# VectorE makes the low part of every weight unit in the GNN groups and Wout

## The chip, the cores and the metric

The kernel runs on one core of a Trainium2 chip, as one program. The metric is the device time of one execution in microseconds (us). The core has five engines with queues of their own: TensorE (PE), VectorE (DVE), ScalarE (ACT), Pool (GpSimd) and the DMA queue of SyncE (SP). They meet only through semaphores.

## The reference

One layer on 384 nodes of 1024 features: a graph attention and a mixing attention run side by side on the same normalised input, and then an attention whose q, k and v come from tree-routed feedforward networks.

```python
xn = layernorm(x)
# gnn: q, k, v = xn @ wq.T + bq ...; q2, k2, v2 = q @ wiq.T + biq ...  (16 heads of 64)
#      softmax(q2 k2^T / 8 + mask(edges)) v2, then @ wo.T + bo
# mix: qkv = xn @ Wqkv; softmax(dots * spiky_weights) v, then @ Wout + bout
x = x + gnn(xn, edges) + mix(xn)
# ffn: three hard-routed trees of 16 leaves give q, k, v; softmax(q k^T / 32) v
x = x + ffn(layernorm(x))
```

## The kernel before

Every matrix product is made from parts of higher and lower significance: an operand a is held as a_hi, a copy rounded to the matmul's input type, and a_lo = a - a_hi, and `product`, `gemm_T` and `gemm_N` add hi*hi, hi*lo and lo*hi.

The weights are a stream of 68 units of 1 MB (128 partitions x 2048 values, 256 output columns each), numbered in the order of use: 24 for the mix groups and the first GNN projections, U_GNN = 24 to 35 for the GNN's second projections (K, Q, V of four groups of four heads), U_OUT = 36 to 39 for Wout, 40 to 43 for wo, and U_FFN = 44 on. Each passes through two-deep buffers, slot n % 2:

- SyncE loads `raw[n % 2]` once the low part of unit n - 2 is made (L335).
- ScalarE's `split_hi(n)` writes `w_hi[n % 2]` (L474); it waits for the load and until TensorE is done with unit n - 1.
- `split_lo(n)` writes `w_lo[n % 2]` = raw - w_hi, on VectorE (L785) for most units, on Pool (L398) for the seven units in ON_POOL: 28, 29, 31, 32, 34, 35 and 37. Two semaphores count, w_lo_ready and w_lo_pool; `lo_turn(n)` is the place of unit n in its count.
- TensorE waits for it in `unit_ready`.

The order of each engine's work is written out by hand. A GNN group gi (0 to 3) begins with the V unit n = U_GNN + 3 gi + 2, and then has four heads. For each head TensorE makes scores (s_bank, L1337), VectorE the masked scores and their maxima (L899, `maxima`), ScalarE the exponentials (L548, `exps`), VectorE the division by the sum (L886, `normals`), TensorE transposes of the three tiles into two banks t_bank (L1346), ScalarE pT_hi (L562) and VectorE pT_lo (L919) from them, and TensorE the product with v (o_bank, L1357), which ScalarE (L570) and VectorE (L850, `join`) bring to o_acc. Between these TensorE makes the K unit n + 1 and the Q unit n + 2 of the next group (in group 3 units 36 and 37 of Wout). `transposes(2)`, the third tile of a head, is issued in the middle of a unit's tile and waits until pT_lo of the first tile has freed its bank of t_bank. `take_K` and `take_Q` bring a unit's results to k_st, q_st and q_lo (ScalarE L498 and L511, VectorE L829 and L841). In group 3 VectorE's `keep_N` copies the results of Wout to y_acc (L964).

ScalarE's order in a group is: exps of head 0, split_hi(n + 1), take_V, exps of head 1, take_V, pT_hi of head 0, exps of head 2, split_hi(n + 2), o_acc of head 0, pT_hi of head 1, exps of head 3, take_K, o_acc, pT_hi of head 2, split_hi(n + 3), take_Q, and so on. VectorE's is the one that the diff shows.

Pool splits the attention outputs beside that: `split_mix(0)` to `(3)`, a cast (L404) and a subtraction (L405) each, and `split_gnn(0)` to `(3)`, two bias additions (L413), a cast (L416) and a subtraction (L417) each, where split_gnn(0) waits until TensorE has done unit 34. Behind split_gnn(2) it issues the loads of bo_b, bout_b, node_raw and b2 (L435 to L438), behind the last head's join the loads of x into x1 (L441); then split_gnn(3), bo_b + bout_b (L445), x1 + bo_b (L447), x1 + y_acc (L450), which sets x1_ready. ScalarE waits for the bias loads before it makes node_hi (L717) and then w_hi of unit 39; VectorE waits for x1_ready, behind split_lo of unit 41 and node_lo (L1120), before it adds the results of wo to x1 (L1129).

Of the kernel before, what the change touches and what calls it, by code (L numbers as in the profile page):

```python
# [24 lines left out]
ALU = mybir.AluOpType  # L25
# [39 lines left out]
def chain_unit(u):  # L65

    return U_A0 if u == 0 else mix_v((u - 1) // 3) + (1, 2, 4)[(u - 1) % 3] if u < 10 else mix_v(3) + u - 9


ON_POOL = (U_GNN + 4, U_GNN + 5, U_GNN + 7, U_GNN + 8, U_GNN + 10, U_GNN + 11, U_OUT + 1)  # L70


def lo_turn(n):

    return sum((u in ON_POOL) == (n in ON_POOL) for u in range(n))


LN_FILLS = KT
# [86 lines left out]
def pv_gnn(g, h):  # L165
    return Index(PV_GNN0 + 4 * g.base + h, g.it, 4 * g.step)
# [24 lines left out]
def program(nc, x, wstream, ecols, pp_in, table, w1m, w2m, bo, bout, nodes, b2, out):  # L191
    with ExitStack() as ctx:
# [12 lines left out]
        def sem(name):  # L205
            return ctx.enter_context(nc.semaphore(name))
# [74 lines left out]
        table_set, table_in, edge_out = sem("table_set"), sem("table_in"), sem("edge_out")  # L281
        raw_in = [sem("raw_in0"), sem("raw_in1")]
        consts_ready = sem("consts_ready")
        w_hi_ready, w_lo_ready, w_lo_pool = sem("w_hi_ready"), sem("w_lo_ready"), sem("w_lo_pool")
        o_half = sem("o_half")
        g_full = sem("g_full")
        g_hi = sem("g_hi")
# [27 lines left out]
        def flat(a):  # L315
            return a.rearrange("p a b -> p (a b)")
# [7 lines left out]
        @block.sync  # L324
        def _(sp):
            for t in range(NT):
                sp.dma_start(x_sb[:, t, :], x[t * P:(t + 1) * P, :]).then_inc(x_in, 16)
            for s in range(2):
                sp.dma_start(raw[:, s, :], wstream[s]).then_inc(raw_in[s], 16)
            for n in range(2, UNITS):  # L330
                if n - 2 in ON_POOL:
                    sp.wait_ge(w_lo_pool, lo_turn(n - 2) + 1)
                else:
                    sp.wait_ge(w_lo_ready, lo_turn(n - 2) + 1)
                sp.dma_start(raw[:, n % 2, :], wstream[n]).then_inc(raw_in[n % 2], 16)  # L335
            for t in range(NT):
                sp.wait_ge(out_ready, 2 * (t + 1))
                sp.dma_start(out[t * P:(t + 1) * P, :], out_sb[:, t, :]).then_inc(out_done, 16)
            sp.wait_ge(out_done, 16 * NT)
# [3 lines left out]
        def _(pool):  # L343
# [49 lines left out]
            pool.wait_ge(g_full, fill_of(Index(mix_v(3) + 1)).value())  # L393
            pool.dma_start(mask8[:, :, :], table.rearrange("(t p m) a -> p t (m a)", t=NT, p=P)).then_inc(table_in, 16)

            def split_lo(n):
                pool.wait_ge(w_hi_ready, n + 1)
                nc.gpsimd.tensor_tensor(flat(w_lo[n % 2][:, :, :]), raw[:, n % 2, :], flat(w_hi[n % 2][:, :, :]),  # L398
                                        ALU.subtract).then_inc(w_lo_pool, 1)

            def split_mix(c):

                both = slice(2 * c, 2 * c + 2)
# [17 lines left out]
            pool.wait_ge(g_full, fill_of(Index(U_GNN)).value())  # L421
            split_mix(0)
            split_mix(1)
            split_lo(U_GNN + 4)
            split_mix(2)
            split_mix(3)
            for n in (U_GNN + 5, U_GNN + 7, U_GNN + 8, U_GNN + 10, U_GNN + 11):
                split_lo(n)
            pool.wait_ge(g_full, fill_of(Index(U_GNN + 11)).value())
            split_gnn(0)  # L430
            split_lo(U_OUT + 1)
            split_gnn(1)
            split_gnn(2)
            pool.wait_ge(g_full, fill_of(Index(U_OUT)).value())
# [339 lines left out]
        def _(dve):  # L774
# [296 lines left out]
            for gi in range(GROUPS):  # L1071
                g = Index(gi)
                n = Index(U_GNN + 3 * gi + 2)
                more = gi < GROUPS - 1
                maxima("gnn", g, 0)
                if gi:
                    join(Index(gi - 1), HG - 1, pv_gnn(Index(gi - 1), HG - 1))
                normals("gnn", g, 0)
                split_lo(n + 1)
                take_V(n, 0)  # L1080
                maxima("gnn", g, 1)
                take_V(n, 1)
                normals("gnn", g, 1)
                take_pT(lambda t: t_gnn(g, 0, t))
                maxima("gnn", g, 2)
                normals("gnn", g, 2)
                join(g, 0, pv_gnn(g, 0))
                if not more:
                    keep_N(n + 1, 0)
                take_pT(lambda t: t_gnn(g, 1, t))  # L1090
                maxima("gnn", g, 3)
                if more:
                    for m in range(2):
                        take_K(n + 1, m, C_BIK + 2 * (gi + 1))
                else:
                    keep_N(n + 1, 1)
                normals("gnn", g, 3)
                join(g, 1, pv_gnn(g, 1))
                take_pT(lambda t: t_gnn(g, 2, t))
                if not more:  # L1100
                    split_lo(n + 3)
                if more:
                    take_Q(n + 2, 0, C_BIQ + 2 * (gi + 1))
                else:
                    keep_N(n + 2, 0)
                join(g, 2, pv_gnn(g, 2))
                take_pT(lambda t: t_gnn(g, 3, t))
                if more:
                    take_Q(n + 2, 1, C_BIQ + 2 * (gi + 1))
                else:  # L1110
                    keep_N(n + 2, 1)
# [126 lines left out]
        def _(pe):  # L1238
# [7 lines left out]
                return last  # L1246

            def unit_ready(n):
                if n.it is None and n.base in ON_POOL:
                    pe.wait_ge(w_lo_pool, lo_turn(n.base) + 1)  # L1250
                else:
                    pe.wait_ge(w_lo_ready, n.value(1, lo_turn(n.base) + 1 - n.base))

            def taken(f):

# [467 lines left out]
```

## Time and profile before

| | before |
|---|---|
| median of 3 runs | 860.81 us (858.89 to 865.01) |
| profiled execution | 865.43 us, span from first to last instruction 863.7 us |
| mean granted TensorE clock | 0.972 |
| PE busy | 786.6 us, 91% |
| DVE busy | 491.7 us, 57% |
| ACT busy | 375.9 us, 44% |
| POOL busy | 172.3 us, 20% |

The span is that of the profiled execution; 1.7 us of its time lie around it. The shares are means over stages: the mix groups end near 340 us, the GNN groups run to about 524, the output projections to about 587, and the FFN to the end.

### The profile page before, as it was taken

To read this page: it belongs to the slowest core of one execution; us is meant where nothing else is said; L and a number is where in the kernel's file an instruction comes from. 1 tells how busy PE (TensorE), PEld (TensorE's weight loads), DVE (VectorE), ACT (ScalarE), POOL (GpSimd) and SP (SyncE) were. 2 spreads that over 40 slices of the span, in tenths; PEclk is the share of its full clock that TensorE was granted. 3 is DMA by queue.
4 is the path that set the end of the run, shared out by engine and by line. 5 is a ranking of instruction groups with operands and counts; after the bars stand their busy time and mean duration, and the time that the engine had idled before them with its cause. 6 is when DMAs were issued, how large, how long until landed. Compare 5 with 4: busy or idle time off the path is not lost.

```text
span 863.7 us, 12450 instructions
## 1 busy us (share of the span) xinstructions
PE 786.6 (91%) x4838; PEld 747.2 (87%) x4838; DVE 491.7 (57%) x1055; ACT 375.9 (44%) x649; POOL 172.3 (20%) x136
## 2 busy tenths in 40 slices
PE   1888999999999799879888998897999999999997
PEld 1778999999999799878788997895898998999995
DVE  5466774774784576757565675645543453364313
ACT  2443655555555446556657552122333333242310
POOL 3201232222322201150403368700000000000000
PEclk9998999999999899999999999898999999999999
DMA  5212122222222222121121217221232233223001
GB/s 210 93 54 94 49 98 99 98 98 98 98 98 98 77 98 98 50 79 69 49 98 49 98 50 243 93 103 44 98 132 112 98 116 129 97 103 142 0 1 74
DMA packets 13956, 79.57 MB, mean 92 GB/s; under 512 B 3168, under 2 KB 3456, under 8 KB 5184
## 3 DMA queue, kind: packets, MB, share of 16 engines
q1 hardware_dynamic: 10656, 74.45, 23.7%
q0 software_dynamic: 2960, 4.26, 1.7%
q8 instruction: 35, 0.57, 0.3%
q10 hardware_dynamic: 288, 0.14, 0.1%
q14 instruction: 17, 0.14, 0.1%
HBM read 76.66 MB, written 2.19 MB: 91 GB/s over the span
## 4 chain that ended last, share of the span: by engine, by line
PE 48%; DMA 22%; DVE 11%; ACT 9%; issue 7%; POOL 2%; POOLq 0%; SPq 0%; ACTq 0%; DVEq 0%
PE g_bank L1274 28%; DMA edge_table<-ew,eidx 20%; PE g_bank L1301 9%; ACT p_ring L548 3%; ACT w_hi L474 3%; DVE w_lo L785 2%; ACT q_st L511 2%; PE g_bank L1245 2%; PE s_bank L1245 1%; PE t_bank L1346 1%; DVE pT_lo L919 1%; DVE p_ring L886 1%; DVE k_st L829 1%; DVE q_lo L841 1%; PE g_bank L1320 1%
## 5 line engine op out<-in xcount | busy, mean ns | idle before, releaser
L1274 PE MATMUL g_bank<-act_hi,w_hi 128*128 128x384 f32 x640 | 228.0, 356 | 6.9 <-DVE k_st L829 3.6
L1274 PE MATMUL g_bank<-act_hi,w_lo 128*128 128x384 f32 x640 | 218.5, 341 | 0.0
L1274 PE MATMUL g_bank<-act_lo,w_hi 128*128 128x384 f32 x640 | 218.2, 341 | 0.0
L785 DVE TENSOR_TENSOR w_lo<-raw,w_hi 128x2048 fp32r<-128x2048 f32 x61 | 147.9, 2425 | 41.2 <-ACT w_hi L474 40.6
L474 ACT ACTIVATE w_hi<-raw 128x2048 fp32r<-128x2048 f32 x68 | 129.6, 1905 | 39.0 <-PE g_bank L1301 38.9
L1274 PEld LDWEIGHTS g_bank<-act_hi,w_hi 128*128 128x128 f32 x640 | 123.8, 193 | 11.8 <-issue 9.9
L1274 PEld LDWEIGHTS g_bank<-act_lo,w_hi 128*128 128x128 f32 x640 | 123.7, 193 | 0.0
L1274 PEld LDWEIGHTS g_bank<-act_hi,w_lo 128*128 128x128 f32 x640 | 123.2, 192 | 0.0
L388 POOL DMA_INDIRECT edge_table<-ew,eidx x51 | 60.3, 1182 | 153.1 <-DMA edge_table<-ew,eidx 150.0
L919 DVE TENSOR_TENSOR pT_lo<-t_bank,pT_hi 128x384 fp32r<-128x384 f32 x96 | 50.4, 552 | 38.8 <-ACT pT_hi L562 30.5
L1346 PE MATMUL t_bank<-ident,p_ring 128*128 128x128 f32 x288 | 43.3, 277 | 27.8 <-DVE pT_lo L919 24.9
L562 ACT ACTIVATE pT_hi<-t_bank 128x384 fp32r<-128x384 f32 x96 | 43.6, 489 | 50.2 <-PE t_bank L1346 49.7
L1346 PEld LDWEIGHTS t_bank<-ident,p_ring 128*128 128x128 f32 x288 | 33.9, 142 | 34.4 <-issue 20.9
L398 POOL TENSOR_TENSOR w_lo<-raw,w_hi 128x2048 fp32r<-128x2048 f32 x7 | 32.1, 4591 | 114.3 <-ACT w_hi L474 114.3
L1301 PE MATMUL g_bank<-w_hi,act_hi 128*128 128x256 f32 x192 | 54.5, 284 | 0.0
L1301 PE MATMUL g_bank<-w_hi,act_lo 128*128 128x256 f32 x192 | 54.3, 283 | 0.0
L1301 PE MATMUL g_bank<-w_lo,act_hi 128*128 128x256 f32 x192 | 54.2, 283 | 0.0
L552 ACT ACTIVATE p_ring<-s_bank,small 128x384 f32<-128x384 f32 x48 | 31.9, 669 | 30.2 <-DVE small L905 30.2
L1274 PE MATMUL g_bank<-h_hi,w_hi 128*128 128x384 f32 x128 | 44.7, 349 | 0.0
L886 DVE TENSOR_SCALAR p_ring<-p_ring,small 128x384 f32<-128x384 f32 x96 | 41.9, 437 | 3.4
L1274 PE MATMUL g_bank<-h_hi,w_lo 128*128 128x384 f32 x128 | 43.0, 336 | 0.0
L1274 PE MATMUL g_bank<-h_lo,w_hi 128*128 128x384 f32 x128 | 42.8, 334 | 0.0
(226 smaller groups left out, 1571.8 us busy)
## 6 DMA issues: line engine op xcount, KB each, us to landing
raw<-wstream_dram SPq DMA_DIRECT2D x68, 1024.0 KB, 4.8
x_sb<-x_dram SPq DMA_DIRECT2D x3, 512.0 KB, 5.0
x<-x_dram POOLq DMA_DIRECT2D x3, 512.0 KB, 6.5
out_dram<-out_sb SPq DMA_DIRECT2D x3, 512.0 KB, 2.6
edge_table<-ew,eidx POOLq DMA_INDIRECT x51, 2.2
edge_table<-mask POOLq DMA_DIRECT2D x1, 576.0 KB, 5.4
mask<-edge_table POOLq DMA_DIRECT2D x1, 576.0 KB, 4.3
bo_b<-bo_dram POOLq DMA_DIRECT2D x1, 512.0 KB, 5.5
```

The costliest lines, as they stand in the source:

```text
L388: nc.gpsimd.indirect_dma_start(table, bass.IndirectOffsetOnAxis(ap=eidx[:, e:e + 1], axis=0), ew[:, e:e + 1], None, bounds_check=N * N - 1 ...
L398: nc.gpsimd.tensor_tensor(flat(w_lo[n % 2][:, :, :]), raw[:, n % 2, :], flat(w_hi[n % 2][:, :, :]), ALU.subtract).then_inc(w_lo_pool, 1)
L474: nc.scalar.activation(flat(w_hi[s][:, :, :]), raw[:, s, :], ACT.Copy).then_inc(w_hi_ready, 1)
L548: ins = nc.scalar.activation(tile, tile, ACT.Exp, bias=nbias[:, s:s + 1], scale=-1.0, accum_out=esum[:, s:s + 1])
L552: ins = nc.scalar.activation(tile, s_bank[q.slot(3)][:, 0:N], ACT.Exp, bias=nbias[:, s:s + 1], scale=alpha[:, c:c + 1], accum_out=esum[:, ...
L562: nc.scalar.activation(pT_hi[:, :, t * P:(t + 1) * P], t_bank[f.slot(2)][:, 0:N].rearrange("p (m n) -> p m n", n=P), ACT.Copy).then_inc(t_ ...
L785: V.tensor_tensor(flat(w_lo[s][:, :, :]), raw[:, s, :], flat(w_hi[s][:, :, :]), ALU.subtract) \
L886: V.tensor_scalar(ring[:, slot, :], ring[:, slot, :], rsum[:, slot:slot + 1], None, ALU.mult) \
L919: V.tensor_tensor(pT_lo[:, :, cols], t_bank[f.slot(2)][:, 0:N].rearrange("p (m n) -> p m n", n=P), pT_hi[:, :, cols], ALU.subtract).then_i ...
L1274: last = mm(out, w2[a], x2[b], start=k == 0 and a + b == 0, stop=not after and k == KT - 1 and a == 1)
L1301: last = mm(out, x2[a], w2[b], start=k == 0 and a + b == 0, stop=not after and k == KT - 1 and a == 1)
L1346: last = nc.tensor.transpose(t_bank[f.slot(2)][:, m * P:(m + 1) * P], p_ring[:, q.slot(PR), m * P:(m + 1) * P], ident[:, :])
```

## The change

Pool no longer makes any low part. ON_POOL, `lo_turn`, w_lo_pool and Pool's `split_lo` are gone. VectorE gets two calls in each GNN group: `split_lo(n + 2)` behind the normals of head 2 and ahead of the join of head 0, and `split_lo(n + 3)` behind pT_lo of head 2, which it had in group 3 only. SyncE and TensorE wait for one count, w_lo_ready. Pool's other work keeps its order and its waits.

```diff
--- before.py
+++ after.py
@@ -65,14 +65,6 @@
 def chain_unit(u):
 
     return U_A0 if u == 0 else mix_v((u - 1) // 3) + (1, 2, 4)[(u - 1) % 3] if u < 10 else mix_v(3) + u - 9
-
-
-ON_POOL = (U_GNN + 4, U_GNN + 5, U_GNN + 7, U_GNN + 8, U_GNN + 10, U_GNN + 11, U_OUT + 1)
-
-
-def lo_turn(n):
-
-    return sum((u in ON_POOL) == (n in ON_POOL) for u in range(n))
 
 
 LN_FILLS = KT
@@ -281,7 +273,7 @@
         table_set, table_in, edge_out = sem("table_set"), sem("table_in"), sem("edge_out")
         raw_in = [sem("raw_in0"), sem("raw_in1")]
         consts_ready = sem("consts_ready")
-        w_hi_ready, w_lo_ready, w_lo_pool = sem("w_hi_ready"), sem("w_lo_ready"), sem("w_lo_pool")
+        w_hi_ready, w_lo_ready = sem("w_hi_ready"), sem("w_lo_ready")
         o_half = sem("o_half")
         g_full = sem("g_full")
         g_hi = sem("g_hi")
@@ -328,10 +320,7 @@
             for s in range(2):
                 sp.dma_start(raw[:, s, :], wstream[s]).then_inc(raw_in[s], 16)
             for n in range(2, UNITS):
-                if n - 2 in ON_POOL:
-                    sp.wait_ge(w_lo_pool, lo_turn(n - 2) + 1)
-                else:
-                    sp.wait_ge(w_lo_ready, lo_turn(n - 2) + 1)
+                sp.wait_ge(w_lo_ready, n - 1)
                 sp.dma_start(raw[:, n % 2, :], wstream[n]).then_inc(raw_in[n % 2], 16)
             for t in range(NT):
                 sp.wait_ge(out_ready, 2 * (t + 1))
@@ -393,11 +382,6 @@
             pool.wait_ge(g_full, fill_of(Index(mix_v(3) + 1)).value())
             pool.dma_start(mask8[:, :, :], table.rearrange("(t p m) a -> p t (m a)", t=NT, p=P)).then_inc(table_in, 16)
 
-            def split_lo(n):
-                pool.wait_ge(w_hi_ready, n + 1)
-                nc.gpsimd.tensor_tensor(flat(w_lo[n % 2][:, :, :]), raw[:, n % 2, :], flat(w_hi[n % 2][:, :, :]),
-                                        ALU.subtract).then_inc(w_lo_pool, 1)
-
             def split_mix(c):
 
                 both = slice(2 * c, 2 * c + 2)
@@ -421,14 +405,10 @@
             pool.wait_ge(g_full, fill_of(Index(U_GNN)).value())
             split_mix(0)
             split_mix(1)
-            split_lo(U_GNN + 4)
             split_mix(2)
             split_mix(3)
-            for n in (U_GNN + 5, U_GNN + 7, U_GNN + 8, U_GNN + 10, U_GNN + 11):
-                split_lo(n)
             pool.wait_ge(g_full, fill_of(Index(U_GNN + 11)).value())
             split_gnn(0)
-            split_lo(U_OUT + 1)
             split_gnn(1)
             split_gnn(2)
             pool.wait_ge(g_full, fill_of(Index(U_OUT)).value())
@@ -1084,6 +1064,7 @@
                 take_pT(lambda t: t_gnn(g, 0, t))
                 maxima("gnn", g, 2)
                 normals("gnn", g, 2)
+                split_lo(n + 2)
                 join(g, 0, pv_gnn(g, 0))
                 if not more:
                     keep_N(n + 1, 0)
@@ -1097,8 +1078,7 @@
                 normals("gnn", g, 3)
                 join(g, 1, pv_gnn(g, 1))
                 take_pT(lambda t: t_gnn(g, 2, t))
-                if not more:
-                    split_lo(n + 3)
+                split_lo(n + 3)
                 if more:
                     take_Q(n + 2, 0, C_BIQ + 2 * (gi + 1))
                 else:
@@ -1246,10 +1226,7 @@
                 return last
 
             def unit_ready(n):
-                if n.it is None and n.base in ON_POOL:
-                    pe.wait_ge(w_lo_pool, lo_turn(n.base) + 1)
-                else:
-                    pe.wait_ge(w_lo_ready, n.value(1, lo_turn(n.base) + 1 - n.base))
+                pe.wait_ge(w_lo_ready, n.value(1, 1))
 
             def taken(f):
```

## Rows read from the trace of the kernel before

**Rows 1.** Waits of TensorE in 336 to 560 us: sum, times, longest, in us.
```profile
PE t_bank L1346 <- DVE pT_lo L919: 18.5, 13, 2.9
...
PE g_bank L1301 <- DVE y_acc L964: 3.2, 1, 3.2
PE g_bank L1301 <- DVE x L1129: 2.9, 1, 2.9
```

**Rows 2.** The page's groups by line: Pool's w_lo (busy us, mean ns | idle before).
```profile
L398 POOL TENSOR_TENSOR w_lo<-raw,w_hi 128x2048 fp32r<-128x2048 f32 x7 | 32.1, 4591 | 114.3 <-ACT w_hi L474 114.3
```

**Rows 3.** Timelines of ScalarE, VectorE and TensorE in group 2: start, duration, [idle before].
```profile
455.10 1.90 ACT L474 ACTIVATE w_hi<-raw 128x2048 fp32r<-128x2048 f32 x1
...
457.54 0.55 DVE L850 TENSOR_TENSOR o_acc<-o_bank,o_acc 64x384 f32<-64x384 f32 x1 [1.70 <-ACT o_acc L570]
458.06 1.02 DVE L919 TENSOR_TENSOR pT_lo<-t_bank,pT_hi 128x384 fp32r<-128x384 f32 x2
...
458.77 0.52 PE L1346 MATMUL t_bank<-ident,p_ring 128*128 128x128 f32 x3 [0.21 <-DVE pT_lo L919]
```

**Rows 4.** The same place in groups 0, 1, 3; last, one window (0.83: granted clock).
```profile
365.90 1.02 DVE L919 TENSOR_TENSOR pT_lo<-t_bank,pT_hi 128x384 fp32r<-128x384 f32 x2
...
367.28 0.49 PE L1346 MATMUL t_bank<-ident,p_ring 128*128 128x128 f32 x3
...
408.76 1.90 ACT L474 ACTIVATE w_hi<-raw 128x2048 fp32r<-128x2048 f32 x1
...
412.12 1.02 DVE L919 TENSOR_TENSOR pT_lo<-t_bank,pT_hi 128x384 fp32r<-128x384 f32 x2
...
413.63 0.49 PE L1346 MATMUL t_bank<-ident,p_ring 128*128 128x128 f32 x3
...
505.20 0.52 PE L1346 MATMUL t_bank<-ident,p_ring 128*128 128x128 f32 x3 [0.61 <-DVE pT_lo L919]
...
400.00:410.00 10.00, 7.97 (x41) 7.68 (x39) 7.25 (x30) 6.43 (x17) 0.00 (x0) 0.83 0.26 101
```

**Rows 5.** Group 0 behind head 2, ScalarE and VectorE.
```profile
379.04 1.92 ACT L474 ACTIVATE w_hi<-raw 128x2048 fp32r<-128x2048 f32 x1
...
383.23 1.25 DVE L841 SCALAR_TENSOR_TENSOR q_lo<-g_bank,pp,q_st 64x384 fp32r<-64x384 f32 x2 [3.62 <-ACT q_st L511]
```

**Rows 6.** Timeline of Pool, from the end of the mix groups on.
```profile
345.07 1.85 POOL L405 TENSOR_TENSOR oTm_lo<-o_acc,oTm_hi 128x768 fp32r<-128x768 f32 x1
...
484.10 1.86 POOL L417 TENSOR_TENSOR oTg_lo<-o_acc,oTg_hi 128x768 fp32r<-128x768 f32 x1
...
502.98 4.61 POOL L398 TENSOR_TENSOR w_lo<-raw,w_hi 128x2048 fp32r<-128x2048 f32 x1 [17.02 <-ACT w_hi L474]
...
516.29 3.75 POOL L417 TENSOR_TENSOR oTg_lo<-o_acc,oTg_hi 128x768 fp32r<-128x768 f32 x1
...
521.16 0.54 POOL L437 DMA_DIRECT2D node_raw<-nodes_dram  x1
...
526.58 2.47 POOL L413 TENSOR_SCALAR o_acc<-o_acc,pp 128x384 f32<-128x384 f32 x2
...
536.31 8.75 POOL L447 TENSOR_TENSOR x<-x,bo_b 128x3072 f32<-128x3072 f32 x1
...
545.84 6.84 POOL L450 TENSOR_TENSOR x<-x,y_acc 128x3072 f32<-128x3072 f32 x1 [0.78 <-DVE y_acc L964]
```

**Rows 7.** Timeline of VectorE: operations from SBUF to SBUF.
```profile
350.37 2.29 DVE L785 TENSOR_TENSOR w_lo<-raw,w_hi 128x2048 fp32r<-128x2048 f32 x1 [1.19 <-ACT w_hi L474]
...
508.76 0.83 DVE L886 TENSOR_SCALAR p_ring<-p_ring,small 128x384 f32<-128x384 f32 x1
...
515.46 2.90 DVE L785 TENSOR_TENSOR w_lo<-raw,w_hi 128x2048 fp32r<-128x2048 f32 x1 [1.24 <-ACT w_hi L474]
...
547.21 7.62 DVE L785 TENSOR_TENSOR w_lo<-raw,w_hi 128x2048 fp32r<-128x2048 f32 x1 [1.52 <-ACT w_hi L474]
...
554.75 1.38 DVE L1120 TENSOR_TENSOR node_lo<-node_raw,node_hi 128x384 fp32r<-128x384 f32 x1
```

## Prediction

> **What bounds the kernel now.** I read the page first, for where TensorE is not busy, then the waits of TensorE between 336 and 560 us, which is where the seven moved operations lie, and then the timelines of the four engines around each of them. Over the whole span TensorE is 91% busy (the table of the profile section has the shares), but in this stretch its longest sum of waits, 18.5 us in 13 waits, is for VectorE's pT_lo, the last link before the transposes may reuse a bank of t_bank; 3.2 us and 2.9 us are single waits in the two output projections [rows 1]. What the reader is to see: the GNN groups are not bound by matmuls alone. They run at the pace of a chain that goes transposes, ScalarE, VectorE, back to TensorE, and every microsecond that is put in front of a pT_lo moves what follows. The operation that changes hands takes 4.59 us on Pool, seven times, 32.1 us in all; VectorE's own takes 2.29 us when nothing disturbs it [rows 2, 7]. Pool is busy for 20% of the span, so the work that it sheds is worth something only where Pool itself is late. That is in one place, the end of this stretch (below).
>
> **The change part by part.** VectorE gets 7 x 2.29 = 16.0 us of work. The value of w_lo is ready 0.04 + 2.29 us after w_hi instead of 0.1 + 4.6 us, but no row of the waits shows TensorE waiting for one of Pool's seven w_lo, nor SP's next load being late for ScalarE, so the shorter operation by itself gives nothing.
>
> *Three splits behind the third pT_lo of head 2 (units 29, 32, 35).* In group 0 ScalarE ends w_hi at 379.04 + 1.92 = 380.96 and VectorE's next work starts only at 383.23, after an idle time of 3.62 us, because it waits for q_st [rows 5]. The split fits into it: 381.00 + 2.29 = 383.29, so 0.06 us, in three groups 0.1 us. The cover is ScalarE's q_st; without it each would cost 2.3 us. I count zero.
>
> *Four splits behind the normals of head 2 (units 28, 31, 34, 37).* Here VectorE is idle too, but for 1.70 us, and it waits for ScalarE's w_hi and then its 0.5 us o_acc. In group 2 w_hi ends at 455.10 + 1.90 = 457.00, VectorE's join starts at 457.54 and its pT_lo at 458.06, and TensorE, which has waited 0.21 us, goes on at 458.77, 0.71 us after pT_lo started [rows 3]. The split can't use that idle time, since it waits for the same w_hi. It starts when w_hi ends and holds VectorE for 2.29 us, where the join came after 0.54 us: join, keep_N, and both pT_lo move by 2.29 - 0.54 = 1.75 us. Queued behind it are join (ScalarE doesn't wait for it), pT_lo (TensorE's transposes wait), and the maxima of head 3. TensorE has little to spare against that:
> - group 2: it waits already, so the whole 1.75 us.
> - group 3: it waits 0.61 us already [rows 4], the whole 1.75 us.
> - group 0: pT_lo from 365.90 to 367.65, transposes possible at 368.36 instead of 367.28 [rows 4]: 1.08 us.
> - group 1: w_hi ends at 410.66; with the 1.06 us of group 2 and the 1.75 us, pT_lo starts at 413.47 instead of 412.12 and the transposes at 414.18 instead of 413.63 [rows 4]: 0.55 us.
> The last two are smaller because TensorE came late itself, in group 1 with the granted clock at 0.83 in 400 to 410 us [rows 4]. Sum 5.1 us. Behind each comes a chain (transposes, pT_hi, pT_lo, maxima, exps, k_st, the next pT_lo) on whose links TensorE waits again in the same group, so I let all of it through. Ends: 0 us if slack swallows them, 7.0 us if all four cost 1.75.
>
> *Pool's other work moves forward.* Two blocks do. split_mix(2) and (3) no longer wait for w_hi of unit 28 and run right behind split_mix(1), which ends at 345.07 + 1.85 = 346.92, to 352.4 (some 2.75 us each: a cast like the 0.8 us one of split_gnn and the subtraction); split_gnn(1) and (2) no longer stand behind the w_lo at 502.98 and follow split_gnn(0), which ends at 484.10 + 1.86 = 485.96, so they run from 486 to 497 [rows 6]. There they meet VectorE operations between SBUF operands. What this costs is seen at 508 to 520. A VectorE w_lo that comes while Pool is at work waits for the end of Pool's instruction and then goes first: 2.90 us instead of 2.29, and Pool's next takes 3.75 us instead of 1.86. The extreme is at 547.21, where w_lo takes 7.62 us, 5.3 more, until Pool's 6.84 us addition is over. A normal (L886) took 0.83 us against 0.42 [rows 6, 7].
> The Trainium skill, page "SBUF — State Buffer", section "Who interferes with whom", says that the two share a port pair, locked for a whole instruction. For w_lo the trace agrees (the 3.75 and 7.62 us).
> In group 0 the normals have 1.19 us of idle behind them before w_lo at 350.37 [rows 7], which takes up most: 0.2 us (0 to 1.9, the latter if Pool's 1.85 us subtraction gets ahead of w_lo). In group 3 the normals before w_lo of unit 36 and w_lo itself lose 0.6 us, the normals of head 1 about 3 x 0.3 us: 1.5 us (0 to 3.5). In return that overlap leaves 508 to 520: w_lo of unit 38 is 0.6 us shorter there, and TensorE waits for what comes behind it: -0.6 us.
>
> *Delay D of TensorE when the last head ends:* 5.1 + 0.2 + 1.5 - 0.6 + 0.1 = 6.3 us.
>
> *What Pool gives back.* bo_b, bout_b and node_raw are issued at about 498 instead of up to 521.16 [rows 6]. Before, ScalarE waits for node_raw before it makes w_hi of unit 39, w_lo follows, y_acc is queued behind w_lo, and TensorE waits 3.2 us for y_acc [rows 1]. That wait goes. What is late next is Pool. Its x1 loads wait for the last join, which is D later, and behind them stand split_gnn(3), from 526.58, the two bias additions (the long one from 536.31 to 545.06) and the addition of y_acc, to 552.68 [rows 6]. This chain moves by D and has only 0.78 us of idle time in it, which now goes, as y_acc is 3.2 us earlier against it. But the earlier w_lo of units 39 and 41 get between Pool's operations at other points and cost it up to 2 us. Then x1_ready comes between 551.7 + D and 553.7 + D. VectorE's node_lo, before at 554.75 with 1.38 us [rows 7] since it was behind the long w_lo, is next, and the x1 addition after it; TensorE restarts at about 554.9 + D, before at 556.79 [rows 1, 6]. So of 6.1 us of waits only 1.9 us are won (0.3 to 2.4); TensorE then waits some 6 us there.
>
> Net: 6.3 - 1.9 = +4.4 us. From there on the FFN is unchanged. The profiled execution took 865.43 us (span 863.7), so it becomes 869.8; the median of the three runs is 860.81, which gives **865.2 us**. With their spread, 858.89 to 865.01, no change and a change of under 1% (8.6 us) can hardly be told apart.
>
> **The rivals.**
> *The waits go and the splits are free.* If something I don't see covers the four splits (TensorE's matmuls could absorb 1 us here and there, as in groups 0 and 1), D is about zero and the net is -1.9 us, at best -6.1 us if both waits of the output projections vanish: 858.9, down to 854.7. For it: VectorE is only 57% busy, and two of four splits meet a late TensorE. Against: 13 waits for exactly that tile.
> *Slower through the clock.* In 400 to 410 us, which begins with one of the 13 waits, the granted clock was 0.83 of the full 2.4 GHz, so it stood for a third of these 10 us on its lower level of 1.2 GHz, and 1.7 us of full speed were lost [rows 4]. The waits before the transposes of head 1 grow to 1.1, 2.0 and 2.4 us in groups 0, 2 and 3. If each brings such a stretch, 3 x 1.7 = 5.1 us come on top: +9.5 us, 870.3. It decides where these waits get as long as the longest of the present ones, 2.9 us [rows 1]. Against: there are 13 waits of 1.4 us on average in this stretch already, and the mean clock over the span is still 0.972.
> *Slower through the whole lock.* If a normal is held for the whole of a Pool instruction and Pool and VectorE take turns, each normal costs up to one Pool operation (1.25 to 1.85 us) instead of 0.3, w_lo of unit 27 and 36 come 3 us later each, and the next normals 2.5 us: 8.5 us instead of 1.7, net +11.2 us, 872.0. This is what the Trainium skill says, page "SBUF — State Buffer", section "Who interferes with whom", of `tensor_scalar` in a two-port mode. Against: 0.83 us is the longest of 96 [rows 7], and Pool's own L413 took 2.47 us [rows 6], as otherwise.
>
> **How the numbers follow.** Forecast 0.63, free splits 0.13, clock 0.14, lock 0.10. The forecast's own range is 862 to 869.5 (D from 4.4 to 9). The range that leaves out no more than 2 in 10 takes in most of the first rival and of the clock: 859 to 872. Faster by over 1% (below 852.2) is beyond every case: 0.02. Slower by over 1% (above 869.4): the lock, two thirds of the clock, a tail of the forecast: 0.23. Within: 0.75.
>
> **What would show it.** Right: seven more w_lo on VectorE of 2.3 us; in groups 2 and 3 the wait before the transposes of head 1 grows by some 1.7 us; q_lo behind the other three doesn't move; split_gnn(1) and (2) at about 486 to 497 relative to their group, node_raw landed long before w_hi of unit 39, no wait for y_acc, one wait of about 6 us for L1129. Wrong: if TensorE's wait for pT_lo in the stretch doesn't grow from 18.5 us, the main term is wrong; if x1_ready no longer sets the end of the projections, the gain is up to 6 us; if normals take over 1 us, the lock; if the granted clock over the span falls from 0.972, the clock.

## The result, and the profile after

The changed kernel takes 869.29 us (median of 8 runs, 867.56 to 870.98), the kernel before 861.41 us (8 runs, 856.14 to 865.01): ratio 1.0096, 95% interval 1.0069 to 1.0123. It is slower by 7.9 us, between 5.9 and 10.6. The forecast was 4.4 us. The profiled execution took 868.51 us with a span of 866.8 us and a mean granted clock of 0.978; over the eight runs the clock lies between 0.970 and 0.978, with a median of 0.974.

The page after, busy times and the groups of w_lo and of the normals:

```profile
PE 781.0 (90%) x4838; PEld 741.3 (86%) x4838; DVE 514.1 (59%) x1062; ACT 375.5 (43%) x649; POOL 141.0 (16%) x129
...
L765 DVE TENSOR_TENSOR w_lo<-raw,w_hi 128x2048 fp32r<-128x2048 f32 x68 | 162.6, 2391 | 45.1 <-ACT w_hi L454 44.5
...
L866 DVE TENSOR_SCALAR p_ring<-p_ring,small 128x384 f32<-128x384 f32 x96 | 44.8, 467 | 3.4
```

Pool is 31.3 us less busy and VectorE 22.4 us more, although seven splits of 2.29 us are only 16.0 us. The rest is mainly node_lo (7.08 us for 1.38) and the normals (44.8 us for 41.9), which stand behind operations of Pool. The waits of TensorE in 336 to 570 us, as in [rows 1]:

```profile
PE t_bank L1323 <- DVE pT_lo L899: 26.4, 15, 3.6
PE g_bank L1278 <- DVE x L1109: 5.5, 1, 5.5
PE g_bank L1251 <- DVE v_st L798: 1.9, 1, 1.9
```

The wait for pT_lo has grown from 18.5 to 26.4 us, a wait of 1.9 us for v_st is new, the one for y_acc (3.2) is gone, and the one for the x1 addition has grown from 2.9 to 5.5 us.

Where the time went is easiest read from borders in VectorE's timeline: the first L899 (L879 after) of each group, the last join and the first addition to x1. Between them, in us, for the profiled executions of all kernels (the tail is from the last join to the first addition to x1; e1 to e12 are the experiments below, and "split" stands for one split_lo):

```
                 group 0  group 1  group 2  group 3   tail    span
before             46.06    46.35    45.88    39.29   32.46   863.7
after              48.78    46.78    46.79    42.69   30.10   866.8
e1 four splits     50.45    46.80    46.83    43.22   30.10   873.5
e2 three splits    46.55    45.16    45.16    38.66   32.48   862.5
e3 Pool held       46.68    46.81    46.80    40.35   30.10   863.3
e4 split later     48.53    45.34    46.51    43.04   30.09   865.9
e5 held + later    49.01    46.53    45.34    41.90   30.10   862.1
e6 early loads     46.54    45.15    45.18    38.68   30.10   858.9
e7 four twice      51.47    49.73    49.49    46.81   30.09   879.9
e8 three twice     51.08    50.65    50.98    42.68   30.11   878.7
e9 clear           46.20    46.53    46.51    41.81   30.10   865.9
e10 Pool chain     45.90    46.34    45.16    39.24   28.78   856.3
e11 w40 first      46.09    46.35    45.15    38.67   28.15   853.5
e12 later alone    46.30    46.50    45.33    39.28   32.47   859.7
```

Two readings matter. Against the profiled execution of before the four groups lose 7.5 us and the tail gives back 2.4; outside them after is 2.0 us shorter, in stages that the change doesn't touch, so the spans differ by 3.1 us only. And that execution of before was itself held up. In e6, whose groups 1 and 2 are those of before, they take 45.15 and 45.18 us, and in e2 45.16; in before 46.35 and 45.88 us, with a stretch of 3.4 us at the lower clock of 1.2 GHz in each. The windows of e6 (group 1) and of before (in group 1):

```profile
392.20:437.30 45.10, 38.57 (x254) 37.10 (x253) 28.72 (x87) 27.76 (x57) 9.17 (x2) 1.00 0.19 71
```

```profile
406.00:409.40 3.40, 3.40 (x13) 3.40 (x12) 3.29 (x16) 2.45 (x7) 0.00 (x0) 0.50 0.03 7
```

The third number from the end is the granted clock. Such a stretch is not wholly chance. e10, e11 and e12 have one at the same place of group 1 (46.34, 46.35 and 46.50 us), e2 and e6 have none there, and in group 0 all five kernels that leave unit 28 to Pool (before, e2, e6, e10, e11) have one, so that an undisturbed group 0 of theirs is in no trace.

Against 45.16 us for an undisturbed group the change costs 3.6 us in group 0, 1.6 in 1 and in 2. Against the 38.67 us of e2, e6 and e11 it costs 4.0 in group 3, and the tail gives back 2.4: 8.4 us, which is inside the measured interval. For group 0 the 45.16 us are an estimate, taken from groups 1 and 2.

**The four splits at the border of head 2.** Group 2 after, VectorE and TensorE, to be held against [rows 3]:

```profile
459.37 2.29 DVE L765 TENSOR_TENSOR w_lo<-raw,w_hi 128x2048 fp32r<-128x2048 f32 x1 [1.19 <-ACT w_hi L454]
461.58 0.54 DVE L830 TENSOR_TENSOR o_acc<-o_bank,o_acc 64x384 f32<-64x384 f32 x1
462.05 1.00 DVE L899 TENSOR_TENSOR pT_lo<-t_bank,pT_hi 128x384 fp32r<-128x384 f32 x2
...
462.73 0.52 PE L1323 MATMUL t_bank<-ident,p_ring 128*128 128x128 f32 x3 [1.83 <-DVE pT_lo L899]
```

VectorE waits 1.19 us for w_hi, then the split stands before join and pT_lo, and TensorE's wait is 1.83 us where it was 0.21. In group 1 the wait is 1.85 us where there was none, in group 3 it is 2.31 where it was 0.61. In group 0 it is only 0.27, because a stretch at the lower clock (0.50 in 360.8 to 364.2 us) lies just ahead and TensorE comes late itself; in e3, which has no such stretch there, it is 1.83.

**The three behind head 2.** Group 0 after, VectorE, against [rows 5]:

```profile
382.90 2.29 DVE L765 TENSOR_TENSOR w_lo<-raw,w_hi 128x2048 fp32r<-128x2048 f32 x1 [1.39 <-ACT w_hi L454]
385.14 1.25 DVE L821 SCALAR_TENSOR_TENSOR q_lo<-g_bank,pp,q_st 64x384 fp32r<-64x384 f32 x2
```

The split and its wait (1.39 + 2.29 us) fill the 3.62 us of idle time that stood before q_lo, and q_lo starts as the split ends.

**Pool and VectorE meet.** Start of group 0 after, VectorE, then Pool:

```profile
347.38 1.82 DVE L866 TENSOR_SCALAR p_ring<-p_ring,small 128x384 f32<-128x384 f32 x1
...
349.31 0.79 DVE L866 TENSOR_SCALAR p_ring<-p_ring,small 128x384 f32<-128x384 f32 x1
350.02 3.94 DVE L765 TENSOR_TENSOR w_lo<-raw,w_hi 128x2048 fp32r<-128x2048 f32 x1
```

```profile
346.97 2.01 POOL L389 TENSOR_TENSOR oTm_lo<-o_acc,oTm_hi 128x768 fp32r<-128x768 f32 x1
348.92 0.96 POOL L388 CAST oTm_hi<-o_acc 128x768 fp32r<-128x768 f32 x1
349.96 1.85 POOL L389 TENSOR_TENSOR oTm_lo<-o_acc,oTm_hi 128x768 fp32r<-128x768 f32 x1
```

A normal of 0.42 us that comes in Pool's subtraction takes 1.82 us, until the subtraction ends. The w_lo at 350.02 comes 0.06 us after Pool's last subtraction has begun and takes 3.94 us: until 351.81, the end of Pool's instruction, it stands, then it runs 2.15 us. At its end VectorE is, counted from the start of the group, 2.1 us behind e3, where Pool is out of the way. In group 3 it is the same with split_gnn(1) and (2), here one line of VectorE:

```profile
500.18 1.78 DVE L866 TENSOR_SCALAR p_ring<-p_ring,small 128x384 f32<-128x384 f32 x1
```

**The tail.** Pool, then VectorE after, against [rows 6, 7]:

```profile
502.86 0.54 POOL L417 DMA_DIRECT2D node_raw<-nodes_dram  x1
...
542.49 8.78 POOL L427 TENSOR_TENSOR x<-x,bo_b 128x3072 f32<-128x3072 f32 x1
551.34 8.65 POOL L430 TENSOR_TENSOR x<-x,y_acc 128x3072 f32<-128x3072 f32 x1
```

```profile
548.94 4.47 DVE L765 TENSOR_TENSOR w_lo<-raw,w_hi 128x2048 fp32r<-128x2048 f32 x1 [1.52 <-ACT w_hi L454]
553.34 7.08 DVE L1100 TENSOR_TENSOR node_lo<-node_raw,node_hi 128x384 fp32r<-128x384 f32 x1
560.34 0.67 DVE L1109 TENSOR_TENSOR x<-x,g_bank 128x512 f32<-128x512 f32 x1
```

node_raw is asked for 27 us before node_hi and w_hi of unit 39 (from 530.23 and 530.66) need it, and the wait for y_acc is gone. Pool's two long additions follow each other without idle time, w_lo of unit 41 gets between them (it ends at 553.41, Pool's addition takes 8.65 us instead of 6.84), and node_lo stands behind the second for 7 us.

### The profile page after: what moved, and what is told of

It reads as the page before. It is cut to its first block, busy times and chain, and to the rows that moved or that the text cites. A ratio compares the mean times of both kernels' runs of the same rounds, so it can differ in the third digit from the quotient of the medians.

```text
span 866.8 us, 12450 instructions
## 1 busy us (share of the span) xinstructions
PE 781.0 (90%) x4838; PEld 741.3 (86%) x4838; DVE 514.1 (59%) x1062; ACT 375.5 (43%) x649; POOL 141.0 (16%) x129
## 4 chain that ended last, share of the span: by engine, by line
PE 48%; DMA 21%; DVE 15%; ACT 8%; issue 7%; POOL 0%; POOLq 0%; SPq 0%; DVEq 0%; ACTq 0%
PE g_bank L1251 27%; DMA edge_table<-ew,eidx 20%; PE g_bank L1278 11%; DVE w_lo L765 4%; ACT w_hi L454 3%; ACT p_ring L528 3%; DVE p_ring L866 2%; PE g_bank L1225 2%; PE s_bank L1225 1%; DVE pT_lo L899 1%; PE t_bank L1323 1%; ACT q_st L491 1%; DVE k_st L809 1%; DVE q_lo L821 1%; PE g_bank L1297 1%
## 5 line engine op out<-in xcount | busy, mean ns | idle before, releaser
L765 DVE TENSOR_TENSOR w_lo<-raw,w_hi 128x2048 fp32r<-128x2048 f32 x68 | 162.6, 2391 | 45.1 <-ACT w_hi L454 44.5
L899 DVE TENSOR_TENSOR pT_lo<-t_bank,pT_hi 128x384 fp32r<-128x384 f32 x96 | 50.3, 551 | 37.9 <-ACT pT_hi L542 29.6
L866 DVE TENSOR_SCALAR p_ring<-p_ring,small 128x384 f32<-128x384 f32 x96 | 44.8, 467 | 3.4
L528 ACT ACTIVATE p_ring<-p_ring,small 128x384 f32<-128x384 f32 x48 | 29.1, 607 | 30.2 <-DVE small L879 30.2
```

Source lines behind the costliest of these rows:

```text
L528: ins = nc.scalar.activation(tile, tile, ACT.Exp, bias=nbias[:, s:s + 1], scale=-1.0, accum_out=esum[:, s:s + 1])
L765: V.tensor_tensor(flat(w_lo[s][:, :, :]), raw[:, s, :], flat(w_hi[s][:, :, :]), ALU.subtract) \
L866: V.tensor_scalar(ring[:, slot, :], ring[:, slot, :], rsum[:, slot:slot + 1], None, ALU.mult) \
L899: V.tensor_tensor(pT_lo[:, :, cols], t_bank[f.slot(2)][:, 0:N].rearrange("p (m n) -> p m n", n=P), pT_hi[:, :, cols], ALU.subtract).then_i ...
```

## Experiments

Each kernel is timed beside the kernel before; the ratios have their 95% intervals behind them.

**e1 and e2: which of the seven.** e1 moves units 28, 31, 34 and 37 to VectorE, e2 units 29, 32 and 35; Pool keeps the others.

```diff
-ON_POOL = (U_GNN + 4, U_GNN + 5, U_GNN + 7, U_GNN + 8, U_GNN + 10, U_GNN + 11, U_OUT + 1)
+ON_POOL = (U_GNN + 5, U_GNN + 8, U_GNN + 11)
...
                 normals("gnn", g, 2)
+                split_lo(n + 2)
```

```diff
-ON_POOL = (U_GNN + 4, U_GNN + 5, U_GNN + 7, U_GNN + 8, U_GNN + 10, U_GNN + 11, U_OUT + 1)
+ON_POOL = (U_GNN + 4, U_GNN + 7, U_GNN + 10, U_OUT + 1)
...
-                if not more:
-                    split_lo(n + 3)
+                split_lo(n + 3)
```

> Units 28, 31, 34 and 37 on VectorE (the four behind the normals of head 2), 29, 32 and 35 stay on Pool. Theory (the delay comes from these four, in the chain to pT_lo, and from Pool's other work that moves forward when unit 28 and 37 leave it): the whole slowdown is here, ratio to before 1.008 to 1.010. Rival (VectorE's extra work as such costs, each split the same): four sevenths of 7.9 us, 4.5 us, ratio 1.005.

> Units 29, 32 and 35 on VectorE (behind pT_lo of head 2), the other four stay on Pool. Theory: hidden under ScalarE's q_st, 0.1 us, ratio 1.000, and in the trace q_lo starts where it did. Rival (each split costs the same): 3.4 us, ratio 1.004.

e1: 1.0103 (1.0086 to 1.0121). e2: 0.9992 (0.9975 to 1.0010). The whole slowdown comes with the four; three more splits on VectorE cost nothing that can be measured. So VectorE's work doesn't cost the same wherever it stands. e1 doesn't part the four splits from Pool's other work, which moves forward with units 28 and 37 (w_lo of unit 27 takes 3.94 us in e1 too); e3 does.

**e3: Pool held back**, the changed kernel with two waits on Pool:

```diff
             split_mix(1)
+            pool.wait_ge(w_lo_ready, U_GNN + 5)
             split_mix(2)
...
             split_gnn(0)
+            pool.wait_ge(w_lo_ready, U_OUT + 2)
             split_gnn(1)
```

> The changed kernel, but Pool waits for w_lo of unit 28 ahead of split_mix(2) and for w_lo of unit 37 ahead of split_gnn(1), so that its work lies about where it lay before (some 2.4 us earlier). Theory: the meetings of Pool with VectorE's normals and w_lo go (2.1 us in group 0 and 3.2 us in group 3), and most of the gain by the early bias loads goes as well; normals and w_lo before group 3 are back at 0.42 and 2.29 us; net 3 us less than the changed kernel, ratio to before 1.005. Rival (meetings don't matter, only the four splits do): loses the early bias loads only, so 1 to 2 us slower than the changed kernel, ratio 1.011.

1.0043 (1.0028 to 1.0058), as the theory had it. The lines of VectorE at the places of the meetings, one normal and w_lo of unit 27, then w_lo of unit 36:

```profile
349.04 0.42 DVE L868 TENSOR_SCALAR p_ring<-p_ring,small 128x384 f32<-128x384 f32 x1
350.64 2.29 DVE L767 TENSOR_TENSOR w_lo<-raw,w_hi 128x2048 fp32r<-128x2048 f32 x1 [1.19 <-ACT w_hi L456]
...
490.93 2.29 DVE L767 TENSOR_TENSOR w_lo<-raw,w_hi 128x2048 fp32r<-128x2048 f32 x1 [0.51 <-ACT w_hi L456]
```

Group 0 falls from 48.78 to 46.68 us and group 3 from 42.69 to 40.35: the meetings cost 2.1 and 2.3 us. One thing was not as expected: the tail stays at 30.10, so the whole give-back is there although Pool's blocks are late again. Against the last join node_raw is asked for 5.0 us earlier than before (7.4 us ahead of it instead of 2.4), and ScalarE had waited 4.65 us for it. The parts summed up in the next section give 3.5 us for e3 (6.5 for the four splits, 0.6 and 2.4 given back), and 3.7 were measured.

**e4: three of the four splits later**, in the changed kernel:

```diff
                 normals("gnn", g, 2)
-                split_lo(n + 2)
+                if not more:
+                    split_lo(n + 2)
...
                 maxima("gnn", g, 3)
                 if more:
+                    split_lo(n + 2)
```

> The changed kernel, with split_lo(n + 2) of groups 0 to 2 moved from behind the normals of head 2 to behind the maxima of head 3, where VectorE is idle for 2.06 us until ScalarE has k_st. Theory: each of the three costs 0.3 us instead of about 1.65 us, 4 us less than the changed kernel, ratio to before 1.004 to 1.005. Rival (VectorE's work as such, or Pool's moved work alone): no difference to the changed kernel, ratio 1.009.

1.0051 (1.0031 to 1.0071). In group 1, VectorE:

```profile
416.77 2.29 DVE L765 TENSOR_TENSOR w_lo<-raw,w_hi 128x2048 fp32r<-128x2048 f32 x1
419.09 2.52 DVE L809 SCALAR_TENSOR_TENSOR k_st<-g_bank,pp,k_st 64x384 fp32r<-64x384 f32 x4
```

The split fills the idle time before k_st, and the group takes 45.34 us: 0.2 us for a split that cost 1.6 us a few instructions earlier. Group 1 is the best of the three. Group 2 has a stretch at the lower clock (from 452.5 us) and takes 46.51 us, and group 0 still has the meeting with Pool and such a stretch as well (48.53 us). Like against like the price holds: in e4, e5, e9 and e12 the later split makes groups 1 and 2 45.33 to 45.34 us without such a stretch and 46.50 to 46.53 with one, against 45.15 to 45.18 and 46.34 to 46.35 in kernels that have no split there. But the 1.6 us are won only in a group without a stretch: 46.5 us is hardly less than the 46.8 of the changed kernel, which the clock doesn't move.

**e5: both edits.** The diffs of e3 and e4 together.

> The changed kernel with both edits of the two runs before: Pool held back, and split_lo(n + 2) of groups 0 to 2 behind the maxima of head 3. Theory (the two causes are separate and add): 0.0043 + 0.0051 - 0.0096 = -0.0002, so ratio to before 0.9998. Rival (they share a part, one edit already took some of the other's): 1.002 to 1.004.

1.0059 (1.0031 to 1.0088): not the theory's 0.9998, and mostly above the rival's range. Group 0 took 49.01 us, and a part of the reason is in its rows, VectorE, then Pool:

```profile
370.56 1.00 DVE L868 TENSOR_SCALAR p_ring<-p_ring,small 128x384 f32<-128x384 f32 x1
...
371.67 1.77 DVE L868 TENSOR_SCALAR p_ring<-p_ring,small 128x384 f32<-128x384 f32 x1
```

```profile
370.52 0.83 POOL L388 CAST oTm_hi<-o_acc 128x768 fp32r<-128x768 f32 x1
371.43 1.80 POOL L389 TENSOR_TENSOR oTm_lo<-o_acc,oTm_hi 128x768 fp32r<-128x768 f32 x1
```

Pool waited for w_lo of unit 28, which now came later, and so met the normals of head 3, which lose 1.9 us. The test was flawed: an edit that was to remove a meeting made another. The clock adds to it, 0.50 in 373.5 to 380.3 us; how much of the 49.01 us each makes is not parted.

**e6: the early loads alone**, on the kernel before; the four loads and the wait ahead of them are gone from behind split_gnn(2).

```diff
             split_gnn(0)
+            pool.wait_ge(g_full, fill_of(Index(U_OUT)).value())
+            pool.dma_start(bo_b[:, :], bo.partition_broadcast(P)).then_inc(bias_in, 16)
+            pool.dma_start(bout_b[:, :], bout.partition_broadcast(P)).then_inc(bias_in, 16)
+            pool.dma_start(node_raw[:, :, :], nodes).then_inc(bias_in, 16)
+            pool.dma_start(b2_raw01[:, :, :], b2[:, 0:2, :]).then_inc(x1_in, 16)
             split_lo(U_OUT + 1)
             split_gnn(1)
```

> The kernel before, unit 37 still on Pool, with one edit: the bias loads and node_raw are issued ahead of Pool's w_lo of unit 37. Theory (the give-back of the changed kernel by itself, Pool's chain is next): the 3.2 us wait for y_acc goes, the wait for L1129 grows, net 1.9 us faster, ratio 0.998. Rival (Pool's lateness was these loads alone): both waits go, 6 us, ratio 0.993.

0.9958 (0.9940 to 0.9976), 3.6 us; the tail shrinks by 2.36 us to the 30.10 of the changed kernel, and the wait for the x1 addition grows as there:

```profile
PE g_bank L1301 <- DVE x L1129: 5.5, 1, 5.5
```

So the give-back is these loads alone, and Pool's chain is next behind them. The 2.4 us of the tail lie within the interval of the ratio (2.1 to 5.2 us); the theory's ratio of 0.998 lies just outside it. Some of the rest goes with the clock, whose median was 0.980 in e6 and 0.976 in the runs of before beside it.

**e7 and e8: double.** In the changed kernel each split_lo(n + 2) is done twice (e7), or each split_lo(n + 3) of groups 0 to 2 (e8); the first result is overwritten by the same values.

```diff
             def split_lo(n, twice=False):
...
+                if twice:
+                    own.done(V.tensor_tensor(flat(w_lo[s][:, :, :]), raw[:, s, :], flat(w_hi[s][:, :, :]), ALU.subtract))
```

> The changed kernel, each split_lo(n + 2) done twice on VectorE (the first result is overwritten by the same values): four more operations of 2.29 us in front of join and pT_lo. Theory (all that stands there passes through to the end): 4 x 2.3 = 9.2 us more than the changed kernel, ratio to before 1.020. Rival (the cost is that of one wait, TensorE's slack takes more): 1.010 to 1.013.

> The changed kernel, split_lo(n + 3) of groups 0 to 2 done twice on VectorE. Theory (the idle time under q_st is just filled by one, w_lo ends as q_lo starts): 3 x 2.3 = 6.9 us more, ratio to before 1.0175. Rival (VectorE or TensorE has slack left there): 1.010 to 1.013.

e7: 1.0232 (1.0205 to 1.0259), e8: 1.0213 (1.0186 to 1.0240). Taken from the changed kernel's 1.0096 that is 11.7 and 10.1 us for 9.2 and 6.9 expected. Both differences carry the intervals of two ratios, together some 3.3 us either way, so the ratios alone don't show the excess. The four groups of the traces do: they grow by 12.5 us in e7 and by 10.3 in e8. Nothing is absorbed, and the cover behind head 2, which makes one split free, is used up by it. The excess goes with the granted clock. The windows of e7 and of the changed kernel (the third number from the end is the clock):

```profile
420.00:430.00 10.00, 9.20 (x44) 9.20 (x45) 6.41 (x21) 5.95 (x14) 0.00 (x0) 0.73 0.28 106
```

```profile
420.00:430.00 10.00, 6.98 (x43) 6.45 (x42) 6.48 (x15) 6.32 (x11) 0.00 (x0) 1.00 0.00 0
```

Over the span the clock was 0.965 in e7 and 0.970 in e8, against 0.978; over all runs the medians are 0.962, 0.969 and 0.974. With still longer waits of TensorE more stretches are at 1.2 GHz. That the waits bring them about fits, but no run sets the one without the other.

**e9: all on VectorE, without the meetings.** e4 with the early loads of e6, and Pool's blocks placed by VectorE's work:

```diff
             split_mix(1)
+            pool.wait_ge(p_ready, s_of("gnn", Index(0), 3, 2).value(1, 1))
             split_mix(2)
...
+            pool.wait_ge(w_lo_ready, U_OUT + 2)
             split_gnn(1)
+            pool.wait_ge(p_ready, s_of("gnn", Index(3), 3, 2).value(1, 1))
             split_gnn(2)
```

> All low parts on VectorE as in the changed kernel, split_lo(n + 2) of groups 0 to 2 behind the maxima of head 3, the bias loads issued right behind split_gnn(0), and Pool's split_mix(2), (3) held until VectorE has done the normals of head 3 of group 0, split_gnn(1) until w_lo of unit 37, split_gnn(2) until the normals of head 3 of group 3: where VectorE has little between SBUF operands. Theory (the two causes are separate; the run that held Pool and moved the splits only traded one meeting for another, with the normals of head 3 of group 0): groups 0, 1 and 2 within 0.5 us of 45.2, group 3 at 40.3, the tail at 30.1; ratio to before 0.999 to 1.001. Rival (the two edits don't add): 1.004 to 1.006 again, with group 0 over 47.

1.0052 (1.0032 to 1.0072), a miss. In group 0 (46.20 us) the meetings with the normals are gone, but the held block made another one, which costs w_lo of unit 29 1.0 us. VectorE, then Pool:

```profile
382.67 3.28 DVE L768 TENSOR_TENSOR w_lo<-raw,w_hi 128x2048 fp32r<-128x2048 f32 x1 [1.38 <-ACT w_hi L457]
```

```profile
381.98 1.83 POOL L389 TENSOR_TENSOR oTm_lo<-o_acc,oTm_hi 128x768 fp32r<-128x768 f32 x1
```

Groups 1 and 2 took 46.5 us and group 3 41.8. The windows show the lower clock in groups 1, 2 and 3, each with 0.83 or 0.88:

```profile
400.00:410.00 10.00, 7.97 (x51) 7.68 (x50) 7.59 (x26) 3.59 (x11) 0.00 (x0) 0.88 0.31 105
455.00:465.00 10.00, 10.00 (x54) 9.94 (x53) 6.22 (x25) 5.64 (x13) 0.00 (x0) 0.83 0.01 2
505.00:515.00 10.00, 7.70 (x48) 7.49 (x47) 6.70 (x17) 5.10 (x11) 5.13 (x4) 0.83 0.30 105
```

**e12: the later place by itself**, on the kernel before: units 28, 31 and 34 on VectorE behind the maxima of head 3, split_mix(2) and (3) held as in e9, the rest on Pool.

```diff
-ON_POOL = (U_GNN + 4, U_GNN + 5, U_GNN + 7, U_GNN + 8, U_GNN + 10, U_GNN + 11, U_OUT + 1)
+ON_POOL = (U_GNN + 5, U_GNN + 8, U_GNN + 11, U_OUT + 1)
...
             split_mix(1)
-            split_lo(U_GNN + 4)
+            pool.wait_ge(p_ready, s_of("gnn", Index(0), 3, 2).value(1, 1))
             split_mix(2)
...
                 maxima("gnn", g, 3)
                 if more:
+                    split_lo(n + 2)
```

> The kernel before with units 28, 31 and 34 on VectorE behind the maxima of head 3, and Pool's split_mix(2), (3) held until VectorE has done the normals of head 3 of group 0; units 29, 32, 35 and 37 stay on Pool and the bias loads stay late. Theory (at that place a split costs 0.2 to 0.3 us, as group 1 of the run with the later split showed: 45.34 us): 0.5 to 0.9 us in all, ratio 1.0005 to 1.001. Rival (the split costs over 1 us there too in most executions, and the one group was luck): 1.003 to 1.005, which would also explain why the run without meetings stayed 0.5% above the kernel before.

1.0001 (0.9979 to 1.0022), the theory's value. The later place costs nothing that can be measured, so it isn't what held e9 up. What does stays open: of e9's edits only unit 37 on VectorE isn't in e2, e6 or e12, and group 3, where it stands, is 3.1 us above e2's; of that 1.7 us are the split at its old place (40.35 us in e3), the rest fits the lower clock. The runs say something on how often the clock falls: in seven of e9's nine the mean clock is 0.970 to 0.974, in twelve of the fourteen of before beside them 0.975 to 0.978. But e9's two runs at 0.978 took 865.4 and 866.0 us, more than any of the five runs of before at 0.978 (860.5 to 864.5), so the clock is not all of it.

**e10 and e11: from there to a faster kernel**, on e6: bo_b + bout_b behind split_gnn(2), node_lo ahead of w_lo of unit 39; e11 also has Pool start its long addition only behind w_lo of unit 40.

```diff
             split_gnn(2)
+            pool.wait_ge(bias_in, 48)
+            own.done(nc.gpsimd.tensor_tensor(bo_b[:, :], bo_b[:, :], bout_b[:, :], ALU.add))
```

```diff
             pool.wait_ge(x1_in, 80)
+            pool.wait_ge(w_lo_ready, lo_turn(U_OUT + 4) + 1)
```

> The kernel before with its seven splits on Pool, the bias loads ahead of w_lo of unit 37 as in the run that was 0.4% faster, and two edits more: bo_b + bout_b is made behind split_gnn(2) instead of behind split_gnn(3), and VectorE's node_lo ahead of w_lo of unit 39. Theory (Pool's chain from the last join to x1_ready sets the end of the projections): it loses its 2.3 us link, the tail shrinks from 30.1 to about 28, ratio to before 0.993 to 0.994. Rival (w_lo of unit 40 now waits for the whole of Pool's long addition and holds TensorE): tail 30 or more, ratio 0.996.

> The run before (loads early, bo_b + bout_b early, node_lo early) with one wait more on Pool: it starts its long addition x1 + bo_b only when w_lo of unit 40 is made. Theory (in that run w_lo of unit 40 took 8.88 us, behind the whole addition, and TensorE waited 2.9 us for y_acc): w_lo of unit 40 back at 2.3 us, the wait for y_acc gone, x1_ready 1 to 2 us earlier, tail 26.5 to 28, ratio to before 0.991 to 0.992. Rival (Pool's chain only starts later and ends later): no gain, tail 28.8 or more, ratio 0.993 or above.

e10: 855.73 us, 0.9929 (0.9905 to 0.9954). e11: 858.50 us, 0.9955 (0.9934 to 0.9976). Both beat both kernels; between the two the intervals leave it open. e10's ratio is the theory's, but its tail is 28.78, so only 1.3 of the link's 2.3 us are won, because of what its rival named. VectorE, and Pool's addition that it stands behind:

```profile
532.45 8.88 DVE L785 TENSOR_TENSOR w_lo<-raw,w_hi 128x2048 fp32r<-128x2048 f32 x1 [1.52 <-ACT w_hi L474]
```

```profile
532.35 6.83 POOL L447 TENSOR_TENSOR x<-x,bo_b 128x3072 f32<-128x3072 f32 x1
```

w_lo comes 0.1 us after Pool has begun and pays 6.7 us for it; TensorE waits 2.9 us for the y_acc behind it. In e11 Pool waits instead:

```profile
535.34 6.84 POOL L448 TENSOR_TENSOR x<-x,bo_b 128x3072 f32<-128x3072 f32 x1 [2.69 <-DVE w_lo L786]
```

That wait for y_acc goes, but Pool's long addition starts 2.5 us later after the last join, and the tail is 28.15, 0.6 us shorter: most of what one side wins the other gives away. The ratio is the rival's (0.993 or above), the tail lies between the two forecasts.

## Why the prediction was right, and where it was off

The range held the time, and the sign of the working was right; the size was 4.4 us for 7.9. The two terms that cost time were both too low.

- *Three splits behind head 2, zero:* right. e2 measures 0.9992, the rows show q_lo starting at the end of the split (385.14 and 385.19), and e8 shows that the cover is just one split deep.
- *Four splits behind the normals of head 2, 5.1 us:* the mechanism was right, the sum was mis-sized by some 1.5 us. Groups 1 and 2 take 46.8 us for 45.16 undisturbed, 1.6 us each; four make 6.5 us, where the fourth, in group 3, is 1.7 (e3) and that of group 0 is an estimate. The forecast took 0.55 and 1.08 us for groups 1 and 0, because TensorE was late there in the one execution read. That lateness went with stretches at the lower clock just ahead (0.50 in 358.2 to 361.6 and in 406.0 to 409.4 us). Against that execution group 1 did lose only 0.43 us; against one without the stretch it loses 1.6. The chain then let everything through, as assumed (e7).
- *Pool's moved work, 1.7 us, and 0.6 back:* the step that missed by most. The places were right, the price was not: 2.1 us in group 0 (forecast 0.2) and 2.3 us in group 3 (forecast 1.5), so 4.4 us (e3 without them, after with them). The 0.3 us for a normal came from rows where it met Pool's bias additions (0.83 us at most); in Pool's subtractions it takes 1.8 us. And w_lo of unit 27 was taken to win the race for the next Pool operation; it came 0.06 us late and lost 1.7 us, which the prediction had named as the end of its range. The 0.6 us back was right: w_lo of unit 38 takes 2.29 us again, and group 3 of the kernels with the splits on Pool takes 39.2 to 39.3 us where that meeting happens (before, e10, e12) and 38.7 where it doesn't (e2, e6, e11).
- *The give-back, -1.9 us:* right, it was -2.36 us, the same in every kernel with the loads early; Pool's chain was next, w_lo of unit 41 got between Pool's two additions, and TensorE waits 5.5 us (forecast 6).

In sum 6.5 + 4.4 - 0.6 - 2.4 = 7.9 us for 7.9 measured; where the meeting of w_lo of unit 38 isn't in the kernel before, 8.5. That it comes out so closely is partly luck, with an interval from 5.9 to 10.6 us, with group 0 estimated and with a clock that differs from run to run.

Of the rivals, the free splits didn't happen. Of the clock the profile shows nothing (0.978 for 0.972), but the eight runs have a median of 0.974, and before has one of 0.976 beside e1 to e12; these 0.002 are about 1.7 us of full speed, so a small part by the clock can't be ruled out. It did happen where more was put there (e7, e8). The lock was half true: normals and w_lo do stand for whole Pool subtractions and take turns with them, but not all six normals did, so its 8.5 us were 4.4. The Trainium skill's rule in "SBUF — State Buffer", section "Who interferes with whom", that the loser blocks for the whole instruction, holds for w_lo (3.94 and 8.88 us) and for the normals in Pool's subtraction (1.82 us), but not for the normals in Pool's addition of a per-partition value (0.56 to 0.83 us); the prediction trusted that milder row above it. That the two engines take turns is of the rows, not of the page.

## What to carry to other kernels

Moving work to an engine with idle time costs nothing if it lands in a wait that it doesn't share, and most of its length if it waits for the same thing as what it is put before: the same 2.29 us split cost 1.6 us behind the normals, 0.2 us behind the next maxima and nothing measurable under q_st. When an operation leaves an engine, look at what moves forward there and whom it will meet. And before a delay is written off against an engine that was late anyway, see in a second trace whether it is late there too, or late by a stretch at the lower clock that other executions don't have.

## What the runs showed of the hardware

- w_lo and node_lo, VectorE operations with both inputs in SBUF, and Pool's operations on SBUF exclude each other for whole instructions, and the one that waits goes next (w_lo at 515.46 behind Pool's cast, Pool's subtraction at 516.29 behind w_lo, [rows 6, 7]). So 0.06 to 0.1 us of order decide over 1.7 us (350.02) or 6.7 us (532.45).
- VectorE's multiplication by a per-partition value (L886, 0.42 us alone) takes 1.8 us in Pool's subtraction but only 0.56 to 0.83 us in Pool's addition of a per-partition value, which is hardly slowed itself (2.57 us for 2.50 in after). Why is open.
- What a stretch at the lower clock costs depends on who sets the pace. With the split behind the normals of head 2, groups 1 and 2 took 46.78 to 46.83 us in all six cases (after, e1 and e3), with a stretch (group 2 of e3, 0.50 in 452.9 to 456.3 us, and of e1) or without. With none there they took 45.15 to 45.18 us without a stretch and 45.88 to 46.35 with one.
